# FFN weights rounded by a second, casting load instead of by ScalarE, in a five-block transformer layer on one core

## The reference

```python
x = x + layernorm(attention(layernorm(x), W_qkv))     # one head of width 128, softmax over 256 keys
h = silu(lin(n, w1)) * lin(n, w2)                     # n = layernorm(x), 128 -> 512
h = gelu(lin(h, h1)); h = gelu(lin(h, h2))            # 512 -> 512, twice
x = x + layernorm(lin(h, w3))                         # 512 -> 128
```

## Time and profile before

| | |
|---|---|
| median of 3 runs | 144.61 us (144.1 to 144.9) |
| profiled execution | 144.72 us |
| its span, first to last instruction | 142.9 us |
| granted TensorE clock, mean | 0.991 |
| busy: PE, DVE, ACT, POOL | 127.7, 112.7, 113.3, 24.7 us |
| HBM read | 4.14 MB, nearly all in the first 14 us |

### The profile page before, as it was taken

How to read it: one execution, slowest core, us unless ns; L and a number is a source line. 1 busy time by engine, 2 the same in 40 slices (tenths; PEclk the granted TensorE clock), 3 DMA queues, 4 the chain that set the end, 5 groups by cost and what they waited for, 6 DMA issues and landing times.

```text
span 142.9 us, 2559 instructions
## 1 busy us (share of the span) xinstructions
PE 127.7 (89%) x749; PEld 106.7 (75%) x749; DVE 112.7 (79%) x362; ACT 113.3 (79%) x218; POOL 24.7 (17%) x33
## 2 busy tenths in 40 slices
PE   6987977999978999999999999999799999799930
PEld 3766855899975888888868888877578888589820
DVE  1766898999958998998889968958997597597553
ACT  3176998999999874949859996999964999968930
POOL 3400211002500000702000025510002052002301
PEclk9999999999999999999999999999999999999996
DMA  4999000000000000000000000120000002000021
GB/s 125 277 367 366 24 7 0 0 5 2 0 5 0 0 0 7 0 5 0 0 0 0 5 2 0 41 76 0 0 0 5 0 5 73 0 0 7 0 76 37
DMA packets 3857, 5.41 MB, mean 38 GB/s; under 512 B 384, under 2 KB 2560, under 8 KB 3840
## 3 DMA queue, kind: packets, MB, share of 16 engines
q1 hardware_dynamic: 3840, 5.19, 11.1%
HBM read 4.14 MB, written 1.05 MB: 36 GB/s over the span
## 4 chain that ended last, share of the span: by engine, by line
PE 53%; ACT 18%; issue 10%; DVE 8%; DMA 5%; POOL 2%; SPq 2%; POOLq 1%; DVEq 0%; ACTq 0%
PE F L1085 16%; PE F L1091 16%; PE A L916 8%; DMA h_raw<-h 5%; PE F L1049 4%; PE F L1052 3%; ACT a_hi L351 3%; ACT act_full L343 3%; ACT h_hi L371 2%; DVE act_full L666 2%; ACT silu L335 2%; DVE a_lo L578 1%; PE A L992 1%; DVE stats L582 1%; ACT probs L289 1%
## 5 line engine op out<-in xcount | busy, mean ns | idle before, releaser
L578 DVE TENSOR_TENSOR a_lo<-act_full,a_hi 128x512 fp32r<-128x512 f32 (+1 forms) x60 | 34.3, 595 | 6.6 <-ACT act_full L343 5.8
L236 POOL TENSOR_TENSOR rstd<-ve,minus_half 128x4 f32<-128x4 f32 (+1 forms) x20 | 18.9, 949 | 109.5 <-DVE ve L589 89.6
L1085 PE MATMUL F<-a_hi,h_hi 128*128 128x512 f32 (+1 forms) x160 | 37.4, 355 | 0.2 <-DVE act_full L666 0.2
L1091 PE MATMUL F<-a_lo,h_hi 128*128 128x512 f32 (+1 forms) x160 | 36.5, 350 | 0.0
L1091 PEld LDWEIGHTS F<-a_lo,h_hi 128*128 128x128 f32 x160 | 26.8, 189 | 4.2
L1085 PEld LDWEIGHTS F<-a_hi,h_hi 128*128 128x128 f32 x160 | 25.9, 189 | 4.0 <-DVE act_full L666 0.4
L351 ACT ACTIVATE a_hi<-F,sc 128x512 fp32r<-128x512 f32 (+1 forms) x40 | 24.2, 629 | 5.6 <-PE F L1091 5.4
L343 ACT ACTIVATE act_full<-F,sc 128x512 f32<-128x512 f32 (+1 forms) x40 | 24.3, 638 | 0.0
L666 DVE SCALAR_TENSOR_TENSOR act_full<-F,sc,silu 128x512 f32<-128x512 f32 (+1 forms) x20 | 12.5, 640 | 2.4 <-ACT silu L335 2.1
L335 ACT ACTIVATE silu<-F,sc 128x512 f32<-128x512 f32 (+1 forms) x20 | 11.5, 602 | 3.4 <-PE F L1052 3.3
L1049 PE MATMUL F<-x2T_hi,w_hi 128*128 128x512 f32 (+1 forms) x40 | 11.4, 367 | 1.7 <-DVE act_full L666 1.1
(11 more groups left out here) (137 smaller groups left out, 235.4 us busy)
## 6 DMA issues: line engine op xcount, KB each, us to landing
h_raw<-h SPq DMA_DIRECT2D x2, 1024.0 KB, 8.9
xs<-x SPq DMA_DIRECT2D x3, 256.0 KB, 7.9
out<-outs SPq DMA_DIRECT2D x3, 256.0 KB, 2.1
w_raw<-w SPq DMA_DIRECT2D x1, 512.0 KB, 4.9
xs<-x SPq DMA_DIRECT2D x2, 128.0 KB, 5.9
w_raw<-w SPq DMA_DIRECT2D x1, 256.0 KB, 9.2
out<-outs SPq DMA_DIRECT2D x2, 128.0 KB, 1.7
wa_raw<-w_attn SPq DMA_DIRECT2D x1, 192.0 KB, 2.4
```

Source lines behind the costliest of these rows:

```text
L236: nc.gpsimd.tensor_tensor(rstd[:, ln, tiles(b)], ve[:, ln, tiles(b)], minus_half[:, 0:SIZES[b]], ALU.pow).then_inc(rstd_ready[ln], 1)
L578: nc.vector.tensor_tensor(dst, full, hi.bitcast(f32), ALU.subtract).then_inc(done, 1)
L1085: nc.tensor.matmul(out, terms[k][0], terms[k][2], start=(k == 0), stop=False)
L1091: last = [nc.tensor.matmul(out, terms[k][0], terms[k][3], start=False, stop=(k == KT - 1)) for out, terms in groups]
```

## The change

Four casting DMAs, issued by GpSimd, load w12, h1, h2 and w3 a second time from HBM straight into the fp32r tensors; ScalarE's copies (one of w12, four of h1, four of h2, one of w3) are gone. The raw loads on SP stay, for the flags and the branch; the load of the scales now stands ahead of w12's, and w3's ahead of x of blocks 3 and 4. TensorE waits once per weight for the new semaphores. Beside that the helper calls on ACT, DVE, PE and POOL stand in another order; no helper has other arithmetic.

```diff
-            sp.dma_start(w12_raw[:, :], w12).then_inc(w12_loaded, 16)
             sp.dma_start(sc[:, :], scales).then_inc(sc_loaded, 16)
+            sp.dma_start(w12_raw[:, :], w12).then_inc(w12_loaded, 16)
...
+            def round_w12():
+                nc.gpsimd.dma_start(w12_hi[:, :], w12).then_inc(w12_rounded, 16)
+            def round_h1():
+                nc.gpsimd.dma_start(h1_hi[:, :, :], h1.rearrange("(k p) o -> p k o", p=P)).then_inc(h1_rounded, 16)
...
+            round_w3()
             rsqrt(LN_X, 0)
+            round_w12()
             rsqrt(LN_X, 1)
             rsqrt(LN_X, 2)
+            round_h1()
             rsqrt(LN_O, 0)
             rsqrt(LN_X1, 0)
+            round_h2()
             rsqrt(LN_O, 1)
...
-            def weights_high(dst, raw, loaded, split):
-                act.wait_ge(loaded, 16)
-                nc.scalar.activation(dst, raw, ACT.Copy).then_inc(split, 1)
...
                 if b == 0:
-                    pe.wait_ge(w12_split, 1)
+                    pe.wait_ge(w12_rounded, 16)
...
-                    if b == 0:
-                        pe.wait_ge(*((h1_split, k + 1), (h2_split, k + 1), (w3_split, 1))[n])
+                    if b == 0 and k == 0:
+                        pe.wait_ge((h1_rounded, h2_rounded, w3_rounded)[n], 16)
```

More of the change, by code:

```diff
@@ L453, in _ @@
             gelu(A3, 0, 3)
+            silu(1, 0)
+            silu(1, 1)
             exps(2, 0)
@@ L512, in _ @@
             x2T_high(3)
+            gelu(A3, 2, 3)
             v_high(4)
-            gelu(A3, 2, 3)
             gT_high(4)
             silu(3, 0)
+            exps(4, 0)
             silu(3, 1)
-            exps(4, 0)
-            silu(3, 2)
             scaled_yT(2)
             pT_high(4, 0)
+            silu(3, 2)
             silu(3, 3)
@@ L737, in _ @@
             gT_low(1)
-            v_low(0)
             pT_low(0, 0)
+            maxima(1, 0)
+            x_normalised(2)
             squared_sums(0)
-            maxima(1, 0)
-            x_statistics(3)
[L743 to L753, removed]
+            maxima(1, 1)
+            attention_out(0)
+            v_low(1)
+            copy_flags(0)
+            squared_sums(1)
+            x1_block(0)
+            pT_low(1, 0)
+            x1_normalised(0)
+            pT_low(1, 1)
+            x2T_low(0)
+            x_statistics(3)
+            copy_flags(1)
             gate(0, 0)
@@ L774, in _ @@
             x1_normalised(1)
-            v_low(2)
+            x_normalised(3)
+            x2T_low(1)
             gT_low(2)
-            x2T_low(1)
+            low(A3, 0, 0)
+            low(A3, 0, 1)
+            low(A3, 0, 2)
+            gate(1, 0)
             maxima(2, 0)
             maxima(2, 1)
-            x_normalised(3)
-            low(A3, 0, 0)
+            v_low(2)
+            high(A1, 1, 0)
+            gate(1, 1)
+            low(A1, 1, 0)
+            pT_low(2, 0)
             squared_sums(2)
-            pT_low(2, 0)
-            low(A3, 0, 1)
-            low(A3, 0, 2)
+            pT_low(2, 1)
+            high(A1, 1, 1)
+            low(A1, 1, 1)
             low(A3, 0, 3)
-            gate(1, 0)
-            gate(1, 1)
-            high(A1, 1, 0)
-            pT_low(2, 1)
-            low(A1, 1, 0)
             gate(1, 2)
-            high(A1, 1, 1)
             high(A1, 1, 2)
-            low(A1, 1, 1)
-            low(A1, 1, 2)
             gate(1, 3)
             high(A1, 1, 3)
+            low(A1, 1, 2)
             low(A1, 1, 3)
@@ L808, in _ @@
             low(A2, 1, 3)
-            x1_block(2)
-            v_low(3)
+            xT_low(3)
             x1_normalised(2)
+            y_statistics(0)
             low(A3, 1, 0)
             low(A3, 1, 1)
-            x_normalised(4)
+            y_shifts(0)
+            gT_low(3)
             x2T_low(2)
-            gT_low(3)
+            maxima(3, 0)
             low(A3, 1, 2)
             low(A3, 1, 3)
-            maxima(3, 0)
+            maxima(3, 1)
             gate(2, 0)
             gate(2, 1)
+            v_low(3)
             high(A1, 2, 0)
+            x_normalised(4)
+            gate(2, 2)
             high(A1, 2, 1)
+            high(A1, 2, 2)
             low(A1, 2, 0)
-            gate(2, 2)
-            maxima(3, 1)
-            high(A1, 2, 2)
             low(A1, 2, 1)
@@ L844, in _ @@
             xT_low(4)
-            low(A3, 2, 0)
             x1_normalised(3)
             x2T_low(3)
+            low(A3, 2, 0)
             gT_low(4)
+            v_low(4)
             low(A3, 2, 1)
-            v_low(4)
             low(A3, 2, 2)
+            maxima(4, 0)
             gate(3, 0)
-            maxima(4, 0)
+            high(A1, 3, 0)
+            squared_sums(4)
+            low(A3, 2, 3)
+            low(A1, 3, 0)
             gate(3, 1)
-            high(A1, 3, 0)
-            low(A1, 3, 0)
-            low(A3, 2, 3)
             high(A1, 3, 1)
+            pT_low(4, 0)
+            gate(3, 2)
             low(A1, 3, 1)
-            gate(3, 2)
             high(A1, 3, 2)
-            pT_low(4, 0)
             low(A1, 3, 2)
             gate(3, 3)
-            squared_sums(4)
             high(A1, 3, 3)
             low(A1, 3, 3)
+            attention_out(4)
             y_statistics(2)
+            x1_block(4)
+            low(A2, 3, 0)
             y_shifts(2)
-            low(A2, 3, 0)
+            x1_normalised(4)
             low(A2, 3, 1)
-            attention_out(4)
             low(A2, 3, 2)
             low(A2, 3, 3)
-            x1_block(4)
-            x1_normalised(4)
+            shift_x1(4)
+            x2T_low(4)
             low(A3, 3, 0)
@@ L1225, in _ @@
             up(3, 0)
-            up(3, 1)
             scores(4, 0)
             begin(A3, 2, (0,), 3)
-            up(3, 2)
+            up(3, 1)
             end(A3, 2, (0,), 3)
             probs_transposes(4, 0)
+            up(3, 2)
+            y_transposes(2)
             up(3, 3)
-            y_transposes(2)
+            attend(4, 0)
             begin(A1, 3, (0, 1), 3)
-            attend(4, 0)
+            attention_transposes(4)
             end(A1, 3, (0, 1), 3)
```

223 lines of the change are left out of this document (102 added, 121 removed).

## The result

The changed kernel takes 145.49 us (median of 8 runs, 145.08 to 146.09), the kernel before 144.72 in the same comparison (8 runs). The ratio is 1.0058, interval 1.0037 to 1.0080: slower by 0.6%. The forecast was 143.4 and faster at 0.60; the time lies in the range, the sign is wrong. The profiled execution took 145.58 us, 0.86 more than that of before.

A forecast was written before the change was run, and what follows sets the result against it. Past 25 us TensorE's matmul work sets the end, plus 4.16 us of holes and the tail. Start 0.2 + hole at 40.1 0.85 + holes behind 0.2 = 1.25 us gained: 143.4 against the median 144.61; range 141.8 to 145.6.

The forecast's parts named there:

- signs that the prediction had named for its own failure: up(0, 0) starting over 1 us from 25.2, or PE's idle time behind 25 us above 4.2 us.
- The start: Chain up to up(0, 0): 0.2 us earlier, bounds 0.7 earlier and 1.0 later.
- (d): Start: x of block 2 lands up to 13.6 us, VectorE waits up to 1.4; pT_low(0, 0) at 15.6, against 16.08.
- (b): Start: gT's high part waits for w12's low sum, done near 9.4 us; uses up a stall saving of about 0.5.
- (c): Start: without h1's first copy, xT's high part of block 1 runs near 10.6 us, 0.7 earlier.
- The hole at 40.1: TensorE's idle time from 40.1 to 51.5 us: gain 0.85 us, bounds 0 and 1.48.
- The replay: New order replayed with old durations from 40.1 us: A1 of block 1 begins at 50.95, against 51.80 before.
- The holes behind: PE's idle time at 95 to 104 and 121 to 127 us: 0.2 us gained; bounds 0.8 lost, 1.2 gained.
- GpSimd's issues: Each second load's issue holds GpSimd 1.0 us, hidden between the rsqrts; TensorE's new waits cost nothing.
- Rival A: GpSimd's issues, 3 us apiece, delay the first two rsqrts; start 2.1 us later, total 145.7 us; chance 0.18.
- Rival D: VectorE's x_normalised holds up GpSimd's issues of w12 and h2 by 0.6 to 1.1 us; total 143.9; chance 0.05.

The follow-up runs named there:

- addr: The kernel before with only the four fp32r weight declarations moved ahead of the raw ones, as in the changed kernel; 145.64 us, ratio 1.0075.
- addr_back: The changed kernel with the fp32r weight declarations back at the place of the kernel before; 144.88 us, ratio 1.0036.
- new_x2: addr_back with x of block 2 issued on SP ahead of raw h1; 143.88 us, ratio 0.9940.
- after_x2: The changed kernel with only x of block 2 issued on SP ahead of raw h1; 144.68 us, ratio 0.9980.
- dummy_cast: The kernel before with the four second loads added into spare tensors that nothing reads, ScalarE's copies kept; 146.64 us, ratio 1.0145.
- after: The changed kernel itself, first measurement, against the kernel before; 145.49 us, ratio 1.0058.
- after_again: The changed kernel measured a second time, without edits, against the kernel before; 145.74 us, ratio 1.0073.
- after_shift: The changed kernel with 32 free bytes ahead of w12_hi, weights 32 past a multiple of 64 bytes; 145.48 us, ratio 1.0063.
- after_pad: The changed kernel with 32 free bytes behind the scales, weights and activations on multiples of 64 bytes; 145.50 us, ratio 1.0064.
- before_pad: The kernel before with 32 free bytes behind the scales, weights and activations on multiples of 64 bytes; 144.93 us, ratio 1.0018.
- cast_only: The kernel before, its order and addresses kept, with the second loads in place of ScalarE's copies; 144.12 us, ratio 0.9971.
- cast_mid: cast_only with the four fp32r weights declared further back, h1_hi from byte 94,944; 144.03 us, ratio 0.9965.
- cast_end: cast_only with the four fp32r weights declared behind all activations, h1_hi from byte 185,056; 144.06 us, ratio 0.9965.
- cast_x2: cast_only with x of block 2 issued on SP ahead of raw h1; 144.13 us, ratio 0.9956.
- new_x2_sum: new_x2 with w12's low sum moved on ScalarE behind gT's and block 1's xT's high parts; 143.41 us, ratio 0.9892.
- split: new_x2 with h1_hi alone in the low region (byte 18,048) and w12_hi at byte 51,424; 144.29 us, ratio 0.9948.

## Why the prediction was wrong

**The step that failed is one that the prediction does not have.** It counts the matmul work behind 25 us as something "which the change leaves as it is". The diff moves four declarations. I read them as text without effect, and gave their new addresses neither a price nor a bound. They make the 512-column matmuls whose weights lie there 4 ns slower on average: 1.05 us by the distances, 1.1 us by addr alone (0.75% of 144.55, interval 0.7 to 1.5), where nothing but addresses changed. This is the largest of the three parts of the miss, 1.05 of 2.1 us. In the changed kernel 0.3 to 0.6 us of it reach the end (addr_back against the changed kernel, and new_x2 against after_x2), since idle time elsewhere swallows part. None of the signs that the prediction had named for its own failure could show this one: up(0, 0) came in time, and PE's idle time from 25 to 127 us adds up to 4.16 us in the stretches above, against 4.21 in the earlier trace rows. PE is as busy as before and slower at the same work. Without this step the forecast of the sign would still have failed: addr_back stands at 1.0036.

**The start came out as forecast, and that hid the larger loss.** Term (d) had its landing right (up to 13.6, measured 13.45) and pT_low(0, 0) as well (15.6, measured 15.47). The prediction sets this against 16.08 of before and calls it no loss, which is right against before. But the new order could have been earlier still. new_x2 takes the wait away and gives 14.90 there, and 0.8 us at up(0, 0) (24.37 against 25.16 in addr_back). In the time it is 1.4 us at the address of before (1.0036 to 0.9940) and 1.3 us at that of the change (1.0073 to 0.9980). So the late x of block 2 costs the changed kernel more than the addresses do. With both taken back the change is a gain (new_x2, 0.9940, 0.9 us), about two thirds of the forecast. How 0.8 us at up(0, 0) become 1.3 to 1.4 in the medians was not followed. x of block 2 landed 9.86 us after its issue, against 7.95 before, and 9.39 in dummy_cast, where the added loads are the only edit ahead of it. The Trainium skill says that loads from all issuers run on the same 16 engines and interleave (DMA: Bandwidth & Descriptors, Issuing engines are not separate DMA queues). These landings agree. Terms (b) and (c) held: gT's high part at 9.88 for a forecast of 9.4, xT's high part of block 1 at 10.40 for 10.6. up(0, 0) at 25.31 lies inside 25.0 give or take 0.5, with an attend of 0.7 us already done that before did at 26.3. On equal footing the start gained about 0.5, for my 0.2.

**The hole at 40.1** gave nothing of its 0.85, the second part of the miss. The replay's landmarks were nearly right: the wait ahead of probs_transposes(2, 0) is 0.86 (forecast 1.2), the last gelu ends at 40.75 for 41.1, the exps begin at 44.65 for 45.0. But all of these came earlier because the start had. The holes from 26.5 to 51 us add up to 2.1 us (distances over 330 ns, less 232) against 1.8 before. Two were not in the replay: 0.26 at 27.18, where PE waits for VectorE's gate, and 0.53 at 40.07, where up(1, 0) waits for a gelu of A3 to free its bank. Start and hole together gave 0.35, where the sum had 1.05.

**The holes behind**, the third part: 0.2 gained forecast, 0.3 lost measured, inside the bounds. 95 to 104 us is 0.11 worse. A new one is at 115.43, where A2's low product waits for VectorE, which has an x_normalised in front of that low part.

**GpSimd's issues**: 1.0 us forecast, 0.58 to 0.80 measured, all hidden. Rival A falls: it had named the right side by luck, for its place, the first two rsqrts, is untouched (3.91 and 6.76). Rival D falls too. w12's issue at 4.61 and h2's at 23.09 ran beside VectorE's x_normalised (4.67 and 23.17) and took 0.58 and 0.78; the two that did not took 0.73 and 0.80. The Trainium skill describes a lock by which a VectorE instruction that uses both ports keeps GpSimd from writing descriptors (SBUF — State Buffer, SBUF: two separate sides). It is not seen in these four issues; whether x_normalised is such an instruction no run tells.

**What the change is worth, piece by piece.** Loads for copies, in the old order: 0.3% faster. The new order on top, with x of block 2 late: from 0.9971 to 1.0036, 0.65% slower. With x of block 2 early both orders are alike, 0.9956 and 0.9940. The moved declarations: 0.75% slower in the old order; in the new one 0.2 to 0.4% by differences whose intervals touch.

## What to carry to other kernels

Price every line of a diff that moves a tensor, not only those that move an instruction: when the bound is a run of equal matmuls, compare the distance of their starts in both traces before looking for waits. Work taken off an engine that is not late buys nothing in that stretch, and the loads that replace it compete with the ones that the start waits for, so issue first what is needed first. An order that brings work forward makes the input that it needs the new bound; a late load that cost nothing measurable in the old order cost 1.3 to 1.4 us in the new.

## What the runs showed of the hardware

- The distance of starts of 512-column fp32r matmuls depends on where their weights lie in SBUF: 233.2 to 233.7 ns with the weights between bytes 18,048 and 40,608 of a partition (addr, after, after_again, after_shift, after_x2; 232.4 in after_pad), 228.5 to 229.5 with them at byte 43,232 or above (before, before_pad, addr_back, cast_only, dummy_cast, cast_mid, cast_end, cast_x2, new_x2, new_x2_sum). It is a matter of the weight operand (split: 233.4 in A1, 229.2 in A2), and not of the place within 64 bytes. At 256 columns nothing is seen (119.5 before, 119.6 after). Why this region is slower, and where its edge lies above 40 KB or below 18, stays open; what else is read or written at those times was not varied.
- A load with conversion issued by GpSimd held it for 0.58 to 0.80 us, whether it moved 256 KB (0.73), 512 KB (0.58) or 1 MB (0.78 and 0.80), and in the changed kernel's trace 1 MB landed 5.5 and 5.9 us after its issue.
